# Two reorderings in a two-layer attention and expert kernel: relative scores copied ahead of the later statistics, with identity products on TensorE, and attention outputs copied one place earlier

## The chip, the cores and the metric

The kernel runs on one core of a Trainium2 chip. The metric is the device time of one execution in microseconds (us). A core has TensorE (PE: products; PEld are its weight loads), VectorE (DVE), ScalarE (ACT), GpSimd (POOL) and SyncE (SP, which here only issues DMAs). Each engine works through its own instructions in the order in which they are written, and waits at a semaphore where the program says so. What is late on one engine is therefore late for all that stands behind it there.

## The reference

Two layers over x of 4 x 512 tokens, 256 wide; all in float32.

```python
# layer 0: attention with relative positions, 16 heads of 16 (the "first attention")
q, k, v = nx @ Wq.T + bq, ctx @ Wk.T + bk, ctx @ Wv.T + bv
attn = softmax(causal((q @ k.T + skew(q @ Er.T)) / sqrt(16)))
x = x + attn @ v
# layer 0: causal self-attention (the "second attention"), then 8 experts, top 2
...
# layer 1: cross-attention, 16 heads of 64, no mask (the "third attention")
q, k, v = norm(x) @ Wq, ctx @ Wk, ctx @ Wv
x = x + softmax(q @ k.T / 8) @ v @ Wo + bo
# layer 1: 16 experts, top 6
...
```

The inputs are normalised over the 256 features ahead of each part: mean and variance (statistics), square root, reciprocal, and one subtract-and-multiply.

## The kernel before, in words

The order of the instructions on each engine is written out by hand; semaphores tie the engines.

**Opening** (0 to 53 us of the trace). Tokens come in two loads: `X[:, 0:4]` (tiles 0 to 3, the first batch element) and `X[:, 4:]` (the other 12 tiles, `ld["x1"]`). DVE does the statistics of the first four (`stats_a(0, RT)`), ACT the root (`sqrt_a`), DVE normalises into `nrm`, PE turns them with the identity `idf` (`tokens_a`), ACT copies them to `NT`. PE projects queries (`queries_a(0)`, four products of 128x512), ACT writes them to `QPa`. Then come the relative scores of job 0 and job 1 (a job is four heads of one batch element): `rel_scores_a(n, r)` for r = 0 to 3 makes a group of eight short-contraction products of 128, 256, 384 and 512 columns (L838). Each group is copied out by two engines, half each: `rel_copy_first(n, r)` on ACT (semaphore `a_en`) and on DVE (`a_end`), since PE may write group q only when ACT has copied group q-1 and DVE group q-2. SP writes the copies to DRAM and reads them back skewed. Between the two jobs PE makes the keys (`keys_a(0)`) and the next queries (`queries_a(1)`); then values and more tokens; then the loop over 16 jobs, whose first relative scores are at L873.

**Third attention** (1022 to 1600 us). 32 jobs (a pair of heads of one batch element), each of four row blocks `s = 4m + r`, taken in pairs (r = 0 and r = 2). In a pair PE makes scores of two blocks (`scores_c`), turns the weights of the two blocks before (`transposes_c`), and multiplies values of blocks s-6 and s-5 (`values_c`, L1350), with one projection in between (`to_bank`). The values of a job gather in one bank, `OUT1`; ACT copies it to `O1T` (`outputs_c`, L1856). The first values of a job wait for the copy of the job before (`c_ot`). ACT also does the exponentials (`exp_c`, L1798), copies half of the turned weights (L1808, L1812), and from job 7 on, at the end of the first pair of a job, rounds the weights of a later job (`weights_high`: `WK`, `WQ`, now and then `WV` or the context), and in a few jobs a square root (`sqrt_c`, with a load of its function table). POOL takes the low parts from those (L736). With every fourth job the projection out (`project_out`, L1306) reads `O1T`.

Of the kernel before, what the change touches and what calls it, by code (L numbers as in the profile page):

```python
# [13 lines left out]
P = 128  # L14
# [4 lines left out]
TB = T // P  # L19
RT = S // P  # L20
# [182 lines left out]
def build(nc, A, out):  # L203

    with ExitStack() as ctx:
# [147 lines left out]
        idf = place("idf", [P, P], F32)  # L353
# [18 lines left out]
        PD = [ctx.enter_context(nc.psum_tensor(f"PS{i}", [P, 2, 512], F32)) for i in range(4)]  # L372
# [427 lines left out]
        def _(pe):  # L800
            mm = nc.tensor.matmul
# [17 lines left out]
            def tokens_a(i):  # L819
                bank_a(("l", i))  # L820
                pe.wait_ge(ln_sem[0]["nrm"], 2 * i + 2)
                for k in range(DK):
                    for x in range(2):
                        last = nc.tensor.transpose(MB[:, (2 * k + x) * P:(2 * k + x + 1) * P],
                                                   nrm[:, (2 * i + x) % 4, k * P:k * P + P], idf[:])
                last.then_inc(a_mw, 1)
# [104 lines left out]
            def queries_h(bank, m):  # L931
                b, half = divmod(m, 2)
                return project(bank, lambda k: eight_heads(WFs, k, half), lambda k: NT[:, k, b * S:b * S + S], S)

            tokens_a(0)
            tokens_a(1)
            pe.wait_ge(ld["w0"], 16)
            queries_a(0)
            pe.wait_ge(ld["er"], 32 * HQ)
            pe.wait_ge(a_mr, A_AT["q", 0] + 1)  # L940
            for r in range(RT):
                rel_scores_a(0, r)
# [564 lines left out]
        def _(act):  # L1507
# [3 lines left out]
            def sqrt_a(i, tb0, tb1):  # L1511
                act.wait_ge(ln_sem[0]["var"], i + 1)
                af(sd[:, tb0:tb1], mv[:, tb0:tb1, 1], ACT.Sqrt, bias=eps_c[:, 0:1]).then_inc(ln_sem[0]["sd"], 1)
# [93 lines left out]
            tokens_a(1)  # L1607
            act.wait_ge(s_bp, 3)
            queries_a(0)
            sqrt_a(1, RT, TB)  # L1610
            for r in range(RT):
                rel_copy_first(0, r)
            keys_a(0)
            queries_a(1)
            for r in range(RT):
                rel_copy_first(1, r)
            tokens_a(2)
            tokens_a(3)
# [234 lines left out]
            def outputs_c(m):  # L1853
                b, p = divmod(m, HP)
                act.wait_ge(c_pv, m + 1)
                af(O1T[b % 2][:, p, :], OUT1[:], ACT.Copy).then_inc(c_ot, 1)  # L1856

            def from_bank(use):
                kind, i = use
                if kind == "k":  # L1860
                    keys_c(i)
                elif kind == "m":
                    tokens_c(i)
                elif kind == "n":
                    tokens_d(i)

            for s in range(0, NST, 2):
                uses = C_PAIR[s // 2]
                m, r = divmod(s, RT)
                if r == 2 and m >= 2:  # L1870
                    outputs_c(m - 2)
                early = s < 6 or not first_is_late(s)
                exp_c(s)
                if s >= 2:
                    weights_c(s - 2)
                for use in uses[:1] if early else ():
                    from_bank(use)
                exp_c(s + 1)
                for use in () if early else uses[:1]:
                    from_bank(use)  # L1880
                if s >= 2:
                    weights_c(s - 1, [0])
                for use in uses[1:2] if early else ():
                    from_bank(use)
                if s >= 2:
                    weights_c(s - 1, [1])
                for use in uses[2 if early else 1:]:
                    from_bank(use)
                if s in (12, 20, 28):
                    sqrt_c(3, s // 8 + 1, RT * (s // 8), RT * (s // 8) + RT)  # L1890
                b, w = divmod(m - HP - 1, HP)
                if r == 0 and 0 <= b < B and w == 4:
                    sqrt_c(4, b, RT * b, RT * b + RT)
                for use in _weight_splits(m):
                    if r == (2 if use[0] == "nt" else 0):
                        weights_high(use)
                if m == NC1 - 1:
                    for i in range(2 * (r // 2), min(2 * (r // 2) + 2, B - 1)):
                        high_part(i)
            for s in range(NST, NST + 40):  # L1900
                m, r = divmod(s, RT)
# [16 lines left out]
        def _(dve):  # L1918
# [23 lines left out]
            def normalise_a(i):  # L1942
                if i >= 2:
                    dve.wait_ge(a_mw, A_W["l", i - 2] + 1)
                for tb in (2 * i, 2 * i + 1):
                    v.tensor_scalar(nrm[:, tb % 4], X[:, tb], mv[:, tb, 0:1], rstd[:, tb:tb + 1], ALU.subtract, ALU.mult)\
                        .then_inc(ln_sem[0]["nrm"], 1)
# [18 lines left out]
            rstd_a(0, 0, RT)  # L1966
            normalise_a(0)
            normalise_a(1)
            dve.wait_ge(ld["x1"], 16)
            stats_a(RT, TB)  # L1970
            for r in range(RT):
                rel_copy_first(0, r)
            rstd_a(1, RT, TB)
            normalise_a(2)
            normalise_a(3)
            for r in range(RT):
                rel_copy_first(1, r)
            dve.wait_ge(ld["rows0"], 48)

            def values_a(tb):  # L1980
# [687 lines left out]
```

## Time and profile before

| what | value |
|---|---|
| median of 3 runs | 1799.07 us (1798.94 to 1806.17) |
| the profiled execution | 1804.25 us, span 1802.1 us |
| PE busy | 1638.3 us, 91% of the span |
| DVE busy | 1083.9 us, 60% |
| ACT busy | 897.6 us, 50% |
| POOL busy | 353.9 us, 20% |
| mean granted TensorE clock | 0.971 |

The span runs from the first to the last instruction; 2.15 us of the profiled execution lie around it. The profiled execution is 5.18 us over the median. Busy time of PE is modelled, since its products are pipelined.

### The profile page before, as it was taken

How to read it: one execution, taken by the hardware profiler on the slowest of the kernel's cores; microseconds unless marked ns; L12 is line 12 of the kernel's file. 1: busy time of each engine (PE TensorE's matmuls, PEld its weight loads, DVE VectorE, ACT ScalarE, POOL GpSimd, SP SyncE). 2: the span in 40 equal slices, each digit the busy share in tenths (PEclk: the TensorE clock that was granted, in tenths of full speed). 3: DMA queues.
4: the chain of work that ended last, by engine and by line, in shares of the span. 5: the costliest groups of instructions: out<-in, count | busy, mean ns of one | idle time of the engine just before them, and what ended most of it. 6: DMA issues, size and time to landing. Idle time of an engine off the chain costs nothing.

```text
span 1802.1 us, 32539 instructions
## 1 busy us (share of the span) xinstructions
PE 1638.3 (91%) x11152; PEld 1100.4 (61%) x11153; DVE 1083.9 (60%) x2947; ACT 897.6 (50%) x2088; POOL 353.9 (20%) x405
## 2 busy tenths in 40 slices
PE   4898989988888878999999798999999999998998
PEld 1555555543333366999999444566666666567887
DVE  3666677755555455222222587876876867767776
ACT  2788788635555421443334366755765765630000
POOL 0011111102442121111110331243332322110000
PEclk9999999889999896999999899999999999999999
DMA  7687778500000093111112320100010000020001
GB/s 262 232 289 258 262 259 286 171 7 1 1 1 1 1 322 139 35 37 36 36 37 70 97 65 24 53 24 24 30 30 25 19 24 18 13 82 1 1 0 47
DMA packets 74448, 149.63 MB, mean 83 GB/s; under 512 B 7024, under 2 KB 49648, under 8 KB 69840
## 3 DMA queue, kind: packets, MB, share of 16 engines
q1 hardware_dynamic: 70912, 138.64, 22.8%
q0 software_dynamic: 3408, 9.31, 1.9%
q8 instruction: 76, 1.25, 0.3%
q14 instruction: 52, 0.43, 0.1%
HBM read 96.68 MB, written 51.25 MB: 82 GB/s over the span
## 4 chain that ended last, share of the span: by engine, by line
PE 76%; DVE 9%; ACT 8%; issue 4%; DMA 1%; POOL 0%; SPq 0%; another core or an unknown queue 0%; DVEq 0%; ACTq 0%; POOLq 0%
PE PS L1380 9%; PE PS L1217 8%; PE PS L1202 7%; PE PS L806 7%; PE PS L1335 6%; PE PS L1251 5%; PE PS L1350 5%; PE PS L1012 4%; PE PS L1325 4%; PE PS L873 4%; PE PS L895 4%; PE PS L1306 3%; PE PS L906 2%; PE PS L1032 2%; ACT PTf L1671 1%
## 5 line engine op out<-in xcount | busy, mean ns | idle before, releaser
L1798 ACT ACTIVATE P<-PS,nm 128x512 f32<-128x512 f32 x256 | 174.6, 695 | 105.7 <-DVE nm L2383 91.5
L1335 PEld LDWEIGHTS PS<-idf,P 128*128 128x128 f32 x1024 | 116.5, 142 | 98.1 <-issue 64.7
L2084 DVE CUSTOM_DVE_ANT_0 dump<-PS,maskw 128x256 f32<-128x256 f32 (+3 forms) x256 | 114.8, 488 | 91.9 <-PE PS L1017 86.7
L1995 DVE CUSTOM_DVE_ANT_0 SN<-PS,SR 128x128 f32<-128x128 f32 (+3 forms) x256 | 115.3, 488 | 87.6 <-PE PS L877 87.5
L1335 PE MATMUL PS<-idf,P 128*128 128x128 f32 x1024 | 154.1, 280 | 11.9 <-ACT PTb L1808 8.2
L2383 DVE TENSOR_REDUCE nm<-PS 128x2 f32<-128x1024 f32 x128 | 150.5, 1216 | 21.1 <-PE PS L1325 20.8
L1217 PEld LDWEIGHTS PS<-xT,W1c 128*128 128x128 f32 x1248 | 145.3, 192 | 4.2 <-ACT xT L1724 2.3
L1217 PE MATMUL PS<-xT,W1c 128*128 128x128 f32 x1248 | 145.8, 275 | 1.8 <-ACT xT L1724 1.8
L1202 PE MATMUL PS<-EW,hT 128*128 x624 | 141.2, 379 | 0.0
L1012 PE MATMUL PS<-QP,KP 32*128 32x128 f32 (+3 forms) x512 | 107.7, 494 | 36.8 <-ACT PTf L1671 33.5
L1671 ACT ACTIVATE PTf<-PS 128x512 f32<-128x512 f32 (+3 forms) x256 | 97.9, 435 | 83.0 <-PE PS L1012 82.8
L1551 ACT ACTIVATE SN<-SN,nm 128x128 f32<-128x128 f32 (+3 forms) x256 | 128.8, 555 | 7.8 <-DVE nm L1995 7.7
L2274 DVE TENSOR_TENSOR ysb<-PS,fc2b 128x256 f32<-128x256 f32 x39 | 16.6, 425 | 191.1 <-PE PS L1202 191.1
L1350 PE MATMUL PS<-PTb,V 128*64 128x512 f32 x512 | 124.0, 604 | 7.7 <-ACT O1T L1856 7.6
L1724 ACT ACTIVATE xT<-PS,cols 128x128 f32<-128x128 f32 x78 | 31.5, 454 | 198.2 <-PE PS L1192 198.2
L2603 DVE SCALAR_TENSOR_TENSOR X<-PS,gat,X 128x256 f32<-128x256 f32 x224 | 97.1, 479 | 46.0 <-PE PS L1380 45.1
L1202 PEld LDWEIGHTS PS<-EW,hT 128*128 128x128 f32 x624 | 115.6, 190 | 14.7 <-issue 0.4
L2392 DVE TENSOR_SCALAR P<-P,rc 128x512 f32<-128x512 f32 x256 | 119.8, 510 | 4.3
L873 PE MATMUL PS<-ErP,QPa 32*128 32x128 f32 (+3 forms) x448 | 92.7, 486 | 22.6 <-ACT EN L1544 13.4
L877 PE MATMUL PS<-Ka,QPa 32*128 32x512 f32 (+3 forms) x512 | 108.1, 496 | 2.7 <-DVE nm L1995 2.5
L1017 PE MATMUL PS<-KP,QP 32*128 32x384 f32 (+3 forms) x512 | 104.7, 492 | 4.0 <-DVE MX L2084 2.0
L895 PEld LDWEIGHTS PS<-idf,SN 128*128 128x128 f32 x640 | 69.3, 143 | 61.1 <-ACT SN L1551 37.4
(345 smaller groups left out, 3306.7 us busy)
## 6 DMA issues: line engine op xcount, KB each, us to landing
SR<-rel SPq DMA_DIRECT2D x16, 1024.0 KB, 7.4
rel<-EN SPq DMA_DIRECT2D x15, 1024.0 KB, 4.8
SR<-rel SPq DMA_DIRECT2D x16, 768.0 KB, 5.8
rel<-EN SPq DMA_DIRECT2D x15, 768.0 KB, 4.1
SR<-rel SPq DMA_DIRECT2D x16, 512.0 KB, 4.5
EW<-in_fc1T SPq DMA_DIRECT2D x8, 1024.0 KB, 11.6
EW<-in_fc2T SPq DMA_DIRECT2D x8, 1024.0 KB, 12.2
rel<-EN SPq DMA_DIRECT2D x15, 512.0 KB, 3.3
```

Source lines behind the costliest of these rows:

```text
L806: last = mm(bank[0:m, 0:n], w(k), src(k), start=(k == 0), stop=(k == DK - 1))
L873: rel_mm = mm(PD[0][:, i, 0:w], QPa[e // 2 % 3][o:o + HQ8, r * P:r * P + P], ErP[e % 2][o:o + HQ8, S - w:S], start=True, stop=True)
L895: last = nc.tensor.transpose(TRA[i % 2][:, o:o + P], SN[(2 * t + j) % 6][:, c * P:c * P + P], idf[:])
L1012: keys_mm = mm(STB[(2 * s + x) % 3][:, 0:S - c * P], KP[o:o + HQ8, hg, b * S + c * P:b * S + c * P + P], QP[n % 4][o:o + HQ8, c * P:S], st ...
L1202: last = mm(PS[5][:, 0:D], hT[s][:, f, :], EW[:, bass.ds(e, 1), o:o + D].rearrange("p e d -> p (e d)"), start=(f == 0), stop=(f == FK - 1))
L1217: ins = mm(PS[1 + 2 * s + f // 4][:, f % 4 * P:f % 4 * P + P], W1c[s][:, o:o + P], xT[:, k, :], start=(k == 0), stop=(k == DK - 1), skip_g ...
L1335: last = nc.tensor.transpose(TR1[j][:, c * P:c * P + P], P1[s % 4][:, j, c * P:c * P + P], idf[:])
L1350: last = mm(OUT1[o:o + DH1, :], V1[chunk % NV1][:, m % VG, o:o + DH1], PT1[m % 2][:, j, c, :], start=(c == 0), stop=(c == RT - 1), skip_gr ...
L1380: last = mm(PS[tb % 8][:].rearrange("p (e n) -> p e n", e=2), x[:, k, t], w[i][:, :, k, :], start=(n + k == 0), stop=(n + k == len(parts) ...
L1551: af(sn, sn, ACT.Exp, bias=nm[:, (ku + i) % 16:(ku + i) % 16 + 1], scale=-1.0).then_inc(a_ex, 1)
L1798: last = af(P1[s % 4][:, j, :], PD[s % 2][:, j, :], ACT.Exp, bias=nm1[:, s % 4, j:j + 1], accum_out=sm1[:, s % 4, j:j + 1])
L2383: v.tensor_reduce(nm1[:, s % 4, :], PD[s % 2][:], AX.X, ALU.max, negate=True).then_inc(c_max, 1)
```

## The change

Three engines get another order, and PE gets 22 more products, in four places of the opening. Their result goes to a bank that nobody reads.

```diff
@@ TensorE, opening
+            def keep_warm(count):
+                for _ in range(count):
+                    mm(PD[2][:, 0, 0:P], idf[:], idf[:], start=True, stop=True)
+
+            keep_warm(12)
             tokens_a(0)
+            keep_warm(3)
             tokens_a(1)
+            keep_warm(4)
             pe.wait_ge(ld["w0"], 16)
             queries_a(0)
             pe.wait_ge(ld["er"], 32 * HQ)
+            keep_warm(3)
             pe.wait_ge(a_mr, A_AT["q", 0] + 1)
             for r in range(RT):
                 rel_scores_a(0, r)
@@ ScalarE, opening
             queries_a(0)
-            sqrt_a(1, RT, TB)
             for r in range(RT):
                 rel_copy_first(0, r)
             keys_a(0)
             queries_a(1)
-            for r in range(RT):
+            rel_copy_first(1, 0)
+            sqrt_a(1, RT, TB)
+            for r in range(1, RT):
                 rel_copy_first(1, r)
@@ ScalarE, third attention
                 m, r = divmod(s, RT)
-                if r == 2 and m >= 2:
-                    outputs_c(m - 2)
                 early = s < 6 or not first_is_late(s)
...
                 for use in uses[2 if early else 1:]:
                     from_bank(use)
+                if r == 0 and m >= 2:
+                    outputs_c(m - 2)
                 if s in (12, 20, 28):
@@ VectorE, opening
             normalise_a(1)
+            for r in range(RT):
+                rel_copy_first(0, r)
             dve.wait_ge(ld["x1"], 16)
             stats_a(RT, TB)
-            for r in range(RT):
-                rel_copy_first(0, r)
+            rel_copy_first(1, 0)
+            rel_copy_first(1, 1)
             rstd_a(1, RT, TB)
             normalise_a(2)
+            rel_copy_first(1, 2)
             normalise_a(3)
-            for r in range(RT):
-                rel_copy_first(1, r)
+            rel_copy_first(1, 3)
```

On VectorE at the start of the program, before the change, the statistics of twelve tiles (BN_STATS, BN_AGGR) stand ahead of the four copies of job 0's relative scores (EN), and `nrm` ahead of those of job 1 (PTa):

```order
L1946 TENSOR_SCALAR nrm<-X,mv,rstd 128x256 x4
L1932 BN_STATS st<-X 128x6 x12
L1935 BN_AGGR mv<-st 128x2 x12
L1953 COPY EN_55<-PS 128x256
L1953 COPY EN_56<-PS 128x512
L1953 COPY EN_57<-PS 128x768
L1953 COPY EN_58<-PS 128x1024
L1940 RECIPROCAL rstd<-sd 128x12
L1946 TENSOR_SCALAR nrm<-X,mv,rstd 128x256 x4
L1953 COPY PTa_0_79<-PS 128x256
```

The same place of VectorE with the change (lines have moved by ten):

```order
L1956 TENSOR_SCALAR nrm<-X,mv,rstd 128x256 x4
L1963 COPY EN_55<-PS 128x256
L1963 COPY EN_56<-PS 128x512
L1963 COPY EN_57<-PS 128x768
L1963 COPY EN_58<-PS 128x1024
L1942 BN_STATS st<-X 128x6 x12
L1945 BN_AGGR mv<-st 128x2 x12
L1963 COPY PTa_0_79<-PS 128x256
L1963 COPY PTa_1_80<-PS 128x512
L1950 RECIPROCAL rstd<-sd 128x12
L1956 TENSOR_SCALAR nrm<-X,mv,rstd 128x256 x2
L1963 COPY PTa_2_81<-PS 128x768
```

The statistics have moved behind all four copies of job 0 and the normalising between the copies of job 1; nothing is added or gone.

On TensorE at the start of the program, with the change (L824 are the turned tokens, L806 the projections, L838 the relative scores; L938 is new):

```order
L938 MATMUL PS<-idf 128x128 x12
L824 MATMUL PS<-idf,nrm 128x128 x4
L938 MATMUL PS<-idf 128x128 x3
L824 MATMUL PS<-idf,nrm 128x128 x4
L938 MATMUL PS<-idf 128x128 x4
L806 MATMUL PS<-NT,WAq 128x512 x2
L938 MATMUL PS<-idf 128x128 x3
L838 MATMUL PS<-ErP_89,QPa_61 128x128 x4
```

The 22 identity products have come in; all else on TensorE keeps its order.

On ScalarE in the third attention, in a job that has a square root and three weight copies at the end of its first pair, before the change:

```order
L1808 ACTIVATE PTb_211<-PS 128x4x128
L1812 ACTIVATE PTb_211<-PS 128x4x128
L1817 ACT_TABLE_LOAD
L1817 ACTIVATE sd<-mv,eps_c 128x4
L1754 ACTIVATE WK1h<-WK_180 128x256
L1758 ACTIVATE WQ1h<-WQ_186 128x256
L1769 ACTIVATE WVh<-WV 128x1024
L1856 ACTIVATE O1T_213<-PS 128x512
L1798 ACT_TABLE_LOAD
```

The same place with the change:

```order
L1818 ACTIVATE PTb_211<-PS 128x4x128
L1822 ACTIVATE PTb_211<-PS 128x4x128
L1866 ACTIVATE O1T_213<-PS 128x512
L1827 ACT_TABLE_LOAD
L1827 ACTIVATE sd<-mv,eps_c 128x4
L1764 ACTIVATE WK1h<-WK_180 128x256
L1768 ACTIVATE WQ1h<-WQ_186 128x256
L1779 ACTIVATE WVh<-WV 128x1024
L1808 ACT_TABLE_LOAD
```

The copy of the outputs has moved ahead of the table load, the root and the weight copies, and nothing else has; in jobs that have none of these it stands where it stood.

## Rows read from the trace of the kernel before

**Rows 1.** The page: busy time (share of the span) of PE, chain by engine

```profile
PE 1638.3 (91%) x11152; PEld 1100.4 (61%) x11153; DVE 1083.9 (60%) x2947; ACT 897.6 (50%) x2088; POOL 353.9 (20%) x405
...
PE 76%; DVE 9%; ACT 8%; issue 4%; DMA 1%; POOL 0%; SPq 0%; another core or an unknown queue 0%; DVEq 0%; ACTq 0%; POOLq 0%
```

**Rows 2.** Timeline of the opening: start us, us, engine, line, operation [idle before <-releaser]

```profile
9.36 1.09 PE L824 MATMUL PS<-idf,nrm 128*128 128x128 f32 x4 [9.36 <-DVE nrm L1946]
...
13.02 3.75 PE L806 MATMUL PS<-NT,WAq 128*128 128x512 f32 x4 [0.78 <-ACT NT L1517]
...
17.71 0.81 PE L838 MATMUL PS<-ErP,QPa 32*128 32x128 f32 x8 [0.93 <-ACT QPa L1527]
19.79 4.02 DVE L1932 BATCH_NORM_STATS2 st<-X 128x6 f32<-128x256 f32 x12 [9.94 <-DMA X<-in_x]
...
24.67 0.39 DVE L1953 COPY EN<-PS 128x256 f32<-128x256 f32 x1
...
25.41 1.24 PE L838 MATMUL PS<-ErP,QPa 32*128 32x256 f32 x8 [6.90 <-ACT EN L1523]
...
31.98 3.71 PE L806 MATMUL PS<-CTA,WAk 128*128 128x512 f32 x4
...
33.52 1.38 DVE L1946 TENSOR_SCALAR nrm<-X,mv,rstd 128x256 f32<-128x256 f32 x4
...
37.23 1.98 PE L806 MATMUL PS<-NT,WAq 128*128 128x512 f32 x4 [1.54 <-ACT Ka L1533]
...
39.14 0.50 PE L838 MATMUL PS<-ErP,QPa 32*128 32x128 f32 x8
...
44.62 1.13 PE L806 MATMUL PS<-WAv,CTA 128*128 128x256 f32 x4
...
53.25 0.37 PE L873 MATMUL PS<-ErP,QPa 32*128 32x128 f32 x1
```

**Rows 3.** DMA issues of the opening: KB each, median us to landing

```profile
X<-in_x SPq DMA_DIRECT2D x1, 1536.0 KB, 12.3
...
cols<-in_cols SPq DMA_DIRECT2D x1, 17.0 KB, 3.3
```

**Rows 4.** Busy time, granted clock, DMA share by stretch: opening, first attention, routing

```profile
13.00:17.00 4.00, 3.75 (x4) 1.17 (x4) 0.00 (x0) 0.13 (x1) 0.00 (x0) 1.00 1.04 375
...
320.00:340.00 20.00, 17.91 (x125) 9.58 (x126) 13.16 (x48) 13.17 (x24) 3.19 (x5) 0.73 0.63 222
...
692.00:696.00 4.00, 2.21 (x4) 0.38 (x2) 3.79 (x12) 0.00 (x0) 0.00 (x0) 0.72 0.05 16
```

**Rows 5.** Timeline of PE in the routing stage

```profile
688.71 5.47 PE L1177 MATMUL PS<-idf 128*128 128x512 f32 x6
```

**Rows 6.** Waits of PE in the third attention: us in total, times, longest

```profile
PE PS L1350 <- ACT O1T L1856: 7.6, 8, 1.9
```

**Rows 7.** Timeline of PE in the third attention

```profile
1118.46 1.94 PE L1350 MATMUL PS<-PTb,V 128*64 128x512 f32 x8 [0.99 <-ACT O1T L1856]
1121.60 1.07 PE L1335 MATMUL PS<-idf,P 128*128 128x128 f32 x8 [0.61 <-ACT PTb L1808]
...
1266.29 1.94 PE L1350 MATMUL PS<-PTb,V 128*64 128x512 f32 x8 [1.93 <-ACT O1T L1856]
1269.43 0.63 PE L1360 MATMUL PS<-idf,nrm 128*128 128x128 f32 x4 [1.21 <-DVE nrm L2425]
...
1331.30 3.72 PE L1306 MATMUL PS<-WO,O1T 128*128 128x256 f32 x16 [0.56 <-ACT O1T L1856]
...
1581.62 1.94 PE L1350 MATMUL PS<-PTb,V 128*64 128x512 f32 x8 [1.02 <-ACT O1T L1856]
```

**Rows 8.** Timeline of ACT, POOL and DVE around the wait at 1266

```profile
1262.40 1.28 ACT L1817 ACT_TABLE_LOAD   x1
...
1266.47 2.35 POOL L736 TENSOR_TENSOR WVl<-WV,WVh 128x1024 fp32r<-128x1024 f32 x1
...
1266.48 2.48 DVE L2425 TENSOR_SCALAR nrm<-X,mv,rstd 128x256 f32<-128x256 f32 x1
```

## The prediction

> **What bounds the kernel now.** I read the page first: PE is busy for 91% of the span and makes up 76% of the chain that ended last [rows 1]. So whatever takes PE's idle or slow time away, at a place where nothing else is just behind, shortens the whole by as much. Then I read the two stretches that the diff touches.
>
> In the opening (the timeline) the reader is to see one hole and one slow stretch. The hole: the first group of relative scores ends at 17.71 + 0.81 = 18.52, but its copy starts on DVE only at 24.67, because DVE first waits for the late load of X until 19.79 and then does twelve tiles of statistics; PE starts its second group at 25.41 [rows 2]. The slow stretch: the same kind of projection takes 3.75 at 13.02 and 3.71 at 31.98, but 1.98 at 37.23; the first group of relative scores takes 0.81 at 17.71, and 0.50 at 39.14 [rows 2]. That is the lower of the two clock levels (1.2 GHz) up to about 36 us and the upper (2.4 GHz) after it. The granted clock of the stretch 13 to 17 reads 1.00 [rows 4], which those durations contradict; I go by the durations.
>
> In the third attention (waits, then PE's timeline) PE waits 7.6 us in 8 places for the copy of the outputs [rows 6], and at two places 0.56 more for it at the projection out [rows 7] (the row at 1331.30; the other is its like in the next batch element).
>
> **The change part by part.** The sum is made against the profiled execution, 1804.25 (span 1802.1 and 2.15 around it). The median is 5.18 lower. I don't know where in the program the other executions are faster, and subtract the same amounts from the median.
>
> *Copies ahead of the statistics.* DVE's copy needs group 0 (18.52) and nothing else, so it starts near 18.6 instead of 24.67; on ACT the square root that waited for the same statistics is gone from ahead of the copy too. PE's second group then starts near 19.0, not 25.41: **-6.4**. What is late next? The statistics (4.02, and 0.9 more for their averages until the copy at 24.67) now run behind the copy of group 3. That copy starts about 31.98 - 6.4 = 25.6 in slow clock, near 22.5 in fast; the load has landed at 19.79 in any case [rows 2, 3]. They end near 28.8 in the fast case, when DVE is wanted for job 1's first copy at about 28.5: **+0.2**. The normalising (1.38 for four tiles, so 0.7 for two [rows 2]) goes into DVE's gaps between copies of job 1, where DVE waits for PE: 0. If these gaps were gone it would cost 1.4 and the reciprocal. The square root is one short ACT instruction in such a gap. SP's order is unchanged; each write and read of the relative scores moves earlier with its copy. They share the DMA engines with the end of the load of X; the cover is that what they bring is first used in the loop at 53.25, behind the values and tokens that begin at 44.62, and both move by the same amount.
>
> *The identity products.* The 22 cost at most 1.09 / 4 = 0.27 each at the lower clock, from the four tokens turned at 9.36 [rows 2]. The first twelve (3.2 us) can start when `idf` and `cols` are in, 1.84 (when SP issued `cols`) + 3.3 = 5.2 [rows 3], and end at 8.5, ahead of 9.36: 0. Three between the tokens take 0.8 where PE idled about 0.7 (the second tokens ran from 13.02 - 0.78 - 1.09 = 11.15, the first to 10.45); four ahead of the queries 1.1 against 0.78; three after them 0.8 against 0.93 [rows 2]. Exposed at the lower clock 0.4, at the upper nothing: **+0.2**.
>
> *What they give back.* The trace has no such products at this place, so I bound it. Below: the clock does not rise before the point where it does now, and they give nothing. Above: it is high from 13.02 on. Then the projection saves 3.75 - 1.98 = 1.8. The four groups of job 0 take, without the hole, 1.3 (0.81, a copy of 0.39 and the signals) + (31.98 - 25.41) = 7.9 at the lower level, and those of job 1 take 44.62 - 39.14 = 5.5 at the upper: 2.4 saved. The keys save 3.71 - 1.98 = 1.7 [rows 2]. Together 5.9. The nearest row for when it rises is the routing stage: six identity products of 512 columns run from 688.71 for 5.47, and the granted clock of 692 to 696 is 0.72, so it was 0.5 and rose to 1.0 within that stretch, near 694.2: about 5.5 us after they began [rows 4, 5]. With the change PE has work from 9.36 almost without a gap to 16.8, after 3 us of work before. I take the rise at about 15, half of the projection's share: **-0.9 - 2.4 - 1.7 = -5.0**. Opening in all: -6.4 + 0.2 + 0.2 - 5.0 = **-11.0**; the loop starts near 42.2 instead of 53.25.
> The Trainium skill, "TensorE: Matmul & The Clock Gate", Part 1, says that the slow state is the default which activity releases, and that how many slow products come first differs between executions of the same kernel. By that rule some executions would get the whole 5.9 and some little of it; the sum would be -11.9 to -6. The trace shows a single execution and can't say.
>
> *The outputs' copy.* It now stands ahead of the table load at 1262.40 instead of behind it and the weight copies [rows 8]. It never has to wait there: the weight copy before it already needs PE to be past those values. ACT does the same work between the same two points, so the exponentials come when they came. So only waits with no ACT or DVE wait close behind are won. Of the 7.6 in 8 places, the one at 1118 (0.99) is followed by 0.61 for the turned weights, which hang on the exponentials: that wait just grows. A second such place, in the last batch element, is counted the same. The one at 1266 (1.93, and its like one batch element on) is followed by 1.21 for `nrm` [rows 7]. `nrm` took 2.48 on DVE from 1266.48, beside a POOL subtraction from 1266.47 for 2.35, where 0.35 is usual [rows 2, 8]: it is released at the same time, so PE idles the full 3.1 all the same. This leaves 7.6 - 2 x 0.99 - 2 x 1.93 - 1.02 = 0.7 in three short waits, won whole; of the 1.02 at 1581 I take 0.7, since DVE goes on only after the router's products that stand behind it on PE; and the 2 x 0.56 at the projection out are won: **-2.5**. Bounds: 0 and -8.7 (all ten).
> The Trainium skill, "SBUF — State Buffer", section "SBUF: two separate sides", says that DVE (in its two-port modes) and GpSimd take one shared port pair as an exclusive lock for a whole instruction. By that rule the trace agrees at 1266; if `nrm` were not held, the copy's move would give some 4 us more, near -6.5.
> POOL's inputs come 0.6 later from ACT, but POOL still has the low parts of keys and queries ahead of them: 0.
>
> *Sum:* -11.0 - 2.5 = -13.5: 1790.8 for an execution like the profiled one, 1785.6 from the median. As the faster executions may already lack a little of the slow clock, I say **1786**.
>
> **The rivals.**
> A, *the clock does not rise early.* For it: 13.02 to 16.77 is solid work and didn't raise it [rows 2]. Against it: that was 3.75 us, now it is over 7. Then 6.4 - 0.4 + 2.5 = 8.5 saved: 1790.6.
> B, *the third attention gives nothing*, since PE's short waits turn up again at the next exponential: 11.0 saved, 1788.
> C, *the waits give more*: DVE gets ahead of POOL by the 0.01 us that part them at 1266 [rows 8], 2 us at each of two places: 1782.
> D, *slower*: all later work stands 11 us earlier, and the first attention sits where the clock may fall: in 320 to 340 the grant is 0.73, so 10.8 of 20 us were at the lower level, about 5.4 us lost [rows 4]. If more stretches fall, each costs half its length. From 1786 it would take 45 us more at the lower level to come out over 1808; nothing in the change points there, as PE's work in the loop is the same. One such stretch more gives 1791.
>
> **How the numbers follow.** Chances: the forecast 0.55 (1782 to 1789), A 0.19, B 0.13, C 0.08, D 0.05 (0.03 of it over 1808). About 0.5%, 9 us, is what a measurement of this kernel can tell from no change: faster means under 1790.1. The forecast, C and most of B are faster, A splits at that line (0.06 under), and of all these some 0.03 is lost to a stretch of lower clock: 0.77 faster, 0.20 same, 0.03 slower. The range goes from C less some clock, 1780, to A plus a stretch of lower clock, 1793.5.
>
> **What would show it.** Right: DVE's first EN copy at 18 to 19; no statistics ahead of it; keys_a at about 22.5 taking 2.0; L873 first at 41 to 43; L1350 waiting for O1T nearly nowhere, yet the wait for nrm near its old place grown to about 3. Wrong: keys at 3.7 (A); L873 first after 46; PE's waits for PTb grown by what O1T lost (B); a loss of granted clock between 42 and 600 greater than before (D). The forecast fails most likely on the clock term.

## The result and the profile after

The changed kernel takes 1793.62 us (median of 22 executions, 1783.59 to 1801.14), beside 1801.36 us for the kernel before on the same chip: a ratio of 0.9958 [0.9941, 0.9974], or 7.6 us less. Forecast were 13.5 us less. The gain is clear of the noise, and a little over half of what was forecast. Its profiled execution took 1797.7 us, with a span of 1795.6.

The page of the changed kernel, busy time and chain by engine, to set beside [rows 1]:

```profile
PE 1650.4 (92%) x11196; PEld 1111.3 (62%) x11197; DVE 1084.5 (60%) x2947; ACT 896.9 (50%) x2088; POOL 353.5 (20%) x405
...
PE 78%; DVE 10%; ACT 8%; issue 4%; DMA 1%; POOL 0%; SPq 0%; DVEq 0%; ACTq 0%; POOLq 0%
```

PE's busy time has grown by 12.1 us, though the 22 new products take some 7 of them. Busy time that grows under the same work is time at the lower clock: the mean granted clock is 0.960, and was 0.971. (The 0.971 is a little too high, since the record of that execution reads 1.00 up to 40 us, against the durations there. The run that leaves the opening alone has 0.966.)

The timeline of PE in the opening of the changed kernel, beside [rows 2] (start, us, engine, line, operation, idle before and its releaser; L938 are the identity products, and each shows as two records):

```profile
5.15 4.57 PE L938 MATMUL PS<-idf 128*128 128x128 f32 x24 [5.15 <-DMA cols<-in_cols]
9.55 0.60 PE L824 MATMUL PS<-idf,nrm 128*128 128x128 f32 x4
...
12.28 1.96 PE L806 MATMUL PS<-NT,WAq 128*128 128x512 f32 x4
...
16.07 0.71 PE L838 MATMUL PS<-ErP,QPa 32*128 32x256 f32 x8 [0.50 <-ACT EN L1532]
...
19.36 2.09 PE L838 MATMUL PS<-ErP,QPa 32*128 32x512 f32 x8 [0.93 <-ACT EN L1532]
21.39 3.78 PE L806 MATMUL PS<-CTA,WAk 128*128 128x512 f32 x4
26.70 1.98 PE L806 MATMUL PS<-NT,WAq 128*128 128x512 f32 x4 [1.54 <-ACT Ka L1542]
...
33.03 2.09 PE L838 MATMUL PS<-ErP,QPa 32*128 32x512 f32 x8 [0.93 <-ACT PTa L1532]
35.05 2.07 PE L806 MATMUL PS<-WAv,CTA 128*128 128x256 f32 x4
...
48.34 0.57 PE L873 MATMUL PS<-ErP,QPa 32*128 32x128 f32 x1
```

The same opening by stretches (columns: length; busy us and instructions of PE, PEld, DVE, ACT, POOL; granted clock; DMA share; GB/s):

```profile
17.00:19.00 2.00, 0.93 (x8) 0.31 (x8) 1.05 (x2) 0.95 (x2) 0.00 (x0) 0.95 1.10 348
19.00:21.00 2.00, 1.64 (x8) 0.52 (x8) 0.46 (x1) 0.31 (x1) 0.00 (x0) 0.50 0.97 191
...
27.00:31.00 4.00, 2.83 (x20) 1.00 (x18) 1.51 (x12) 1.63 (x4) 0.35 (x1) 1.00 0.95 342
...
35.00:50.00 15.00, 11.63 (x40) 7.00 (x40) 4.90 (x13) 3.00 (x5) 1.27 (x2) 0.50 0.69 245
```

The hole is gone: the second group starts at 16.07 instead of 25.41. The clock rises before 9.55 (the turned tokens take 0.60, against 1.09 before), earlier than I thought. But it falls twice: by 19.36 (2.09 for the last group of job 0, where 1.14 is usual at the upper level, then keys 3.78), and again by 33.03, and from 35 to 50 it reads 0.50. There the four projections of values take 2.07 each, where the kernel before needed 1.13. The loop starts at 48.34 instead of 53.25: 4.9 us won, not 11.0.

In the third attention the waits for the outputs' copy of [rows 6] are gone. PE's waits for `nrm` have grown. Over the whole run they were 4.2 us in 3 places, the longest 1.8, and are now:

```profile
PE PS L1369 <- DVE nrm L2437: 9.3, 4, 3.2
```

The timelines of ACT, POOL, DVE and PE at the two places that answer to 1266 in [rows 7, 8]:

```profile
1255.53 0.59 ACT L1866 ACTIVATE O1T<-PS 128x512 f32<-128x512 f32 x1
1256.14 1.28 ACT L1827 ACT_TABLE_LOAD   x1
...
1259.71 2.34 POOL L736 TENSOR_TENSOR WVl<-WV,WVh 128x1024 fp32r<-128x1024 f32 x1
...
1259.72 2.81 DVE L2437 TENSOR_SCALAR nrm<-X,mv,rstd 128x256 f32<-128x256 f32 x2
...
1262.67 0.63 PE L1369 MATMUL PS<-idf,nrm 128*128 128x128 f32 x4 [3.20 <-DVE nrm L2437]
...
1405.55 1.09 PE L1369 MATMUL PS<-idf,nrm 128*128 128x128 f32 x4 [3.21 <-DVE nrm L2437]
1406.43 1.91 PE L1344 MATMUL PS<-idf,P 128*128 128x128 f32 x8
```

The copy is early, and PE stands still just as long: 1.93 + 1.21 has become one wait of 3.20, as forecast. The new thing is behind the second one: 1.09 instead of 0.63, and 1.91 for what takes 1.04 behind the first. The clock has fallen: it reads 0.51 over the 6 us behind this wait.

### The profile page after: what moved, and what is told of

Its sections match the earlier page's. It is cut to its first block, busy times and chain, and to the rows that moved or that the text cites. A ratio compares the mean times of both kernels' runs of the same rounds, so it can differ in the third digit from the quotient of the medians.

```text
span 1795.6 us, 32625 instructions
## 1 busy us (share of the span) xinstructions
PE 1650.4 (92%) x11196; PEld 1111.3 (62%) x11197; DVE 1084.5 (60%) x2947; ACT 896.9 (50%) x2088; POOL 353.5 (20%) x405
## 4 chain that ended last, share of the span: by engine, by line
PE 78%; DVE 10%; ACT 8%; issue 4%; DMA 1%; POOL 0%; SPq 0%; DVEq 0%; ACTq 0%; POOLq 0%
PE PS L1389 9%; PE PS L1226 8%; PE PS L806 8%; PE PS L1211 8%; PE PS L1344 6%; PE PS L1260 5%; PE PS L1359 5%; PE PS L1334 5%; PE PS L1021 4%; PE PS L873 4%; PE PS L895 4%; PE PS L1315 3%; PE PS L906 2%; PE PS L1041 2%; ACT PTf L1681 1%
## 5 line engine op out<-in xcount | busy, mean ns | idle before, releaser
L2615 DVE SCALAR_TENSOR_TENSOR X<-PS,gat,X 128x256 f32<-128x256 f32 x224 | 97.1, 479 | 46.1 <-PE PS L1389 45.3
L1359 PE MATMUL PS<-PTb,V 128*64 128x512 f32 x512 | 124.0, 605 | 0.0
L873 PE MATMUL PS<-ErP,QPa 32*128 32x128 f32 (+3 forms) x448 | 93.6, 490 | 23.0 <-ACT EN L1553 13.3
L1026 PE MATMUL PS<-KP,QP 32*128 32x384 f32 (+3 forms) x512 | 104.7, 492 | 4.0 <-DVE MX L2096 2.0
```

Of the source, the lines that this page charges most:

```text
L873: rel_mm = mm(PD[0][:, i, 0:w], QPa[e // 2 % 3][o:o + HQ8, r * P:r * P + P], ErP[e % 2][o:o + HQ8, S - w:S], start=True, stop=True)
L1359: last = mm(OUT1[o:o + DH1, :], V1[chunk % NV1][:, m % VG, o:o + DH1], PT1[m % 2][:, j, c, :], start=(c == 0), stop=(c == RT - 1), skip_gr ...
```

## The experiments

Each kernel is timed beside the kernel before on the same chip. "Loop" is the start of the loop over the 16 jobs, the first product of L873 in the one profiled execution, in us (kernel before: 53.25, and 52.1 in the run that leaves its opening alone, so 52.7 in the mean). The last column is the mean granted clock from 13 to 25 us, 25 to 40 and 40 to 55.

| kernel | ratio, 95% interval | loop | granted clock |
|---|---|---|---|
| changed | 0.9958 [0.9941, 0.9974] | 48.3 | 0.74, 0.73, 0.57 |
| changed, second time | 0.9960 [0.9937, 0.9983] | 42.1 | 0.86, 1.00, 0.89 |
| copies alone | 0.9937 [0.9916, 0.9959] | 45.2 | 0.79, 0.94, 0.89 |
| copies alone, second time | 0.9966 [0.9949, 0.9984] | 44.9 | 0.77, 0.95, 0.89 |
| identity products alone | 0.9997 [0.9979, 1.0016] | 53.5 | 0.83, 0.68, 1.00 |
| outputs alone | 0.9998 [0.9981, 1.0016] | 52.1 | 0.79, 0.71, 0.97 |
| copies and identity products | 0.9958 [0.9933, 0.9984] | 48.5 | 0.76, 0.73, 0.56 |
| copies and outputs | 0.9963 [0.9947, 0.9978] | 44.9 | 0.77, 0.96, 0.89 |
| first half of the gaps filled | 0.9964 [0.9945, 0.9983] | 46.7 | 1.00, 0.70, 0.61 |
| all gaps filled | 0.993 [0.991, 0.995] | 40.4 | 1.00, 1.00, 1.00 |
| all filled, `nrm` earlier | 0.993 [0.9906, 0.9953] | 40.4 | 1.00, 1.00, 1.00 |
| all filled, outputs as before | 0.9924 [0.9905, 0.9943] | 40.6 | 1.00, 1.00, 1.00 |
| changed, WVl in four parts | one execution | 42.3 | 0.86, 1.00, 0.89 |

**Each part alone.** The copies ahead of the statistics, without the other two parts:

```diff
-            keep_warm(12)
             tokens_a(0)
-            keep_warm(3)
             tokens_a(1)
-            keep_warm(4)
...
-            keep_warm(3)
...
+                if r == 2 and m >= 2:
+                    outputs_c(m - 2)
...
-                if r == 0 and m >= 2:
-                    outputs_c(m - 2)
```

> The opening's new order on DVE and ACT, without the 22 identity products and with the outputs' copy at its old place. Theory 1 (the hole of 6.9 us is what the reordering is worth; the lower clock in the opening costs the rest): the second group of relative scores starts near 19.0 instead of 25.4, the query projection still takes 3.7; first product of the loop near 47, thus 6 us earlier; time ratio about 0.9965. Theory 2 (the identity products are what moves the opening): less than 3 us earlier at the loop, ratio 0.999.

Measured 1795.4 us beside 1804.39, ratio 0.9937. This part carries the whole gain. Its opening, PE's timeline in the second such run (the first is like it: 45.2 and 44.9 at the loop):

```profile
13.01 3.49 PE L806 MATMUL PS<-NT,WAq 128*128 128x512 f32 x4 [0.78 <-ACT NT L1522]
17.43 0.50 PE L838 MATMUL PS<-ErP,QPa 32*128 32x128 f32 x8 [0.93 <-ACT QPa L1532]
18.43 0.71 PE L838 MATMUL PS<-ErP,QPa 32*128 32x256 f32 x8 [0.49 <-ACT EN L1528]
19.86 1.66 PE L838 MATMUL PS<-ErP,QPa 32*128 32x384 f32 x8 [0.72 <-ACT EN L1528]
22.45 2.09 PE L838 MATMUL PS<-ErP,QPa 32*128 32x512 f32 x8 [0.93 <-ACT EN L1528]
24.47 2.90 PE L806 MATMUL PS<-CTA,WAk 128*128 128x512 f32 x4
...
44.94 0.37 PE L873 MATMUL PS<-ErP,QPa 32*128 32x128 f32 x1
```

Here too the clock is up at 17.43 (0.50), without any identity product. It is down by 19.86 (1.66 for a group that takes 0.93 at the upper level), and up again within the keys (2.90, between 1.98 and 3.78). The values run at the upper level. The second timing:

> The reordered copies alone, a second time. Theory 1: the ratio of 0.9937 seen before holds within its interval (0.992 to 0.996) and is not above that of the full change by more than 0.001; loop start 44 to 46.5 us if the clock rises at the same place as before, up to 49 if the level differs between executions as it did with the full change (48.3 and 42.1). Rival (the first result was a lucky draw and the identity products do matter): 0.997 or more.

1794.12 us, 0.9966. The two intervals overlap, and both hold the full change's 0.9958.

The 22 identity products on the order of before:

```diff
+            keep_warm(12)
             tokens_a(0)
+            keep_warm(3)
...
```

> The 22 identity products alone, in the order of the kernel before. Theory 1: the query projection takes 2.0 instead of 3.75, but its 1.8 us are swallowed by the wait for the statistics (the copy stays at 24.7), and the clock falls in that wait of 9 us or more, so that groups 1 to 3 and the keys run at the lower level as before: loop start at 53.2 give or take 1, ratio 1.000. Theory 2: 4 us or more earlier, ratio 0.9975.

Ratio 0.9997, loop at 53.5. PE's timeline around the old hole:

```profile
16.11 0.50 PE L838 MATMUL PS<-ErP,QPa 32*128 32x128 f32 x8 [0.17 <-ACT QPa L1536]
26.65 1.24 PE L838 MATMUL PS<-ErP,QPa 32*128 32x256 f32 x8 [10.03 <-ACT EN L1532]
```

The first group is 1.6 earlier and at the upper level, and behind a hole of 10.03 all of it is lost.

The outputs' copy alone, on ACT only:

```diff
-                if r == 2 and m >= 2:
-                    outputs_c(m - 2)
...
+                if r == 0 and m >= 2:
+                    outputs_c(m - 2)
```

> Only the copy of the outputs moved, the opening as before. Theory 1 (short waits are won, the long ones become a single wait of 3.2 for nrm): waits for O1T gone, waits for nrm up from 2.4 to about 7.5, the third attention 1.8 to 2.5 us shorter if the clock holds, up to 2 less if it falls behind one of the 3.2 us waits; ratio 0.9985 to 1.000. Theory 2 (all ten waits are won): 8 us shorter, ratio 0.9955.

Ratio 0.9998. The waits for O1T are gone and those for `nrm` grow to 9.3 us in 4 places, as in the changed kernel. Nothing is won that the time shows; its interval leaves room for 3.4 us at most.

**Two parts at a time.** The full change without the outputs' part, and without the identity products:

```diff
+                if r == 2 and m >= 2:
+                    outputs_c(m - 2)
...
-                if r == 0 and m >= 2:
-                    outputs_c(m - 2)
```

> The change without its third-attention part: copies ahead of the statistics and the 22 identity products, outputs copied where they were. If the outputs' move is worth nothing (theory 1: its saved waits of 7.6 us come back as a wait for nrm and as lower clock behind it), this equals the full change: ratio 0.994 to 0.997 against before, loop start anywhere from 42 to 48 us, the wait for the outputs' copy again about 7.6 in 8 places, the wait for nrm 2 to 2.4 in 2 places, clock 1.00 behind both. If the move is worth its forecast 2.5 us (rival), this is 0.0014 above the full change's 0.996, which five rounds can hardly tell; if it costs time, this is 2 to 4 us faster, about 0.993.

```diff
-            keep_warm(12)
...
-            keep_warm(3)
...
-            keep_warm(4)
...
-            keep_warm(3)
```

> The change without the identity products. Theory 1 (the reordered copies carry the gain, identity products in these four places add under 2 us): ratio 0.994 to 0.997, loop start 44 to 46.5 us, q projection about 3.7 us at the lower clock, keys either level. Rival (the identity products carry the clock part of the forecast, 5.0 us): 0.998 to 0.999 here.

The ratios are 0.9958 and 0.9963, each the same as the full change within its interval. Neither the identity products nor the outputs add anything that can be measured to the copies.

**The same kernel again.** The changed kernel was timed and profiled a second time, with no edit.

> The changed kernel once more, unaltered, on another occasion. Theory 1 (after the first fall the clock of the opening is a matter of where the waits lie to the moment at which the clock is reviewed, and so of luck): its opening shows another pattern of falls, and the loop starts anywhere between 43 and 49 (48.3 before). Rival (the pattern belongs to the kernel): loop at 48.3 within 0.3 and the same granted clock in 25 to 40 and 40 to 55 (0.73, 0.57).

Ratio 0.9960, the same. But the profiled execution differs from the first. PE's timeline:

```profile
19.86 2.09 PE L838 MATMUL PS<-ErP,QPa 32*128 32x512 f32 x8 [0.93 <-ACT EN L1532]
21.88 2.67 PE L806 MATMUL PS<-CTA,WAk 128*128 128x512 f32 x4
...
32.41 1.14 PE L838 MATMUL PS<-ErP,QPa 32*128 32x512 f32 x8 [0.93 <-ACT PTa L1532]
33.48 1.13 PE L806 MATMUL PS<-WAv,CTA 128*128 128x256 f32 x4
...
42.10 0.37 PE L873 MATMUL PS<-ErP,QPa 32*128 32x128 f32 x1
```

The same program, the same waits, and another clock. Against the first profile the keys take 2.67 instead of 3.78 (1.1 us), the last group 1.14 instead of 2.09 (0.95), four values 1.13 instead of 2.07 (3.8), and two groups of tokens 0.66 instead of 1.12 (0.9). That is 6.75, less the 0.5 by which this execution was behind at 19.86: the 6.2 between 48.3 and 42.1. Four profiled executions have this opening (the two of the changed kernel, the one of copies and identity products, and the one with WVl in four parts). Their loops start at 48.3, 42.1, 48.5 and 42.3, 45.3 in the mean. The three without identity products (copies alone twice, copies and outputs) start the loop at 45.2, 44.9 and 44.9. So the identity products at these four places bring the clock up sooner, and it then falls at the last group of job 1, ahead of the values, in two profiled executions of four; in the mean they give nothing.

**All gaps filled.** If the clock falls in the idle gaps between the short groups, then more identity products there must keep it. 41 more, into a bank that nobody reads at that time, behind each group but the last of a job, behind the keys, behind each projection of values and between the tokens:

```diff
+            def fill(count):
+                for _ in range(count):
+                    mm(PS[6][:, 0:P], idf[:], idf[:], start=True, stop=True)
...
             for r in range(RT):
                 rel_scores_a(0, r)
+                fill((2, 3, 4, 0)[r])
...
             keys_a(0)
+            fill(7)
             queries_a(1)
             for r in range(RT):
                 rel_scores_a(1, r)
+                fill((3, 3, 4, 0)[r])
...
                 values_to_bank_a(tb)
+                fill(3)
             tokens_a(2)
+            fill(3)
```

> The changed kernel with more identity products, into a bank that nothing reads before the loop, in every gap of PE from the first group of relative scores to the last tokens before the loop (2, 3, 4 behind the groups of job 0, 7 behind the keys, 3, 3, 4 behind those of job 1, 3 behind each of the values, 3 between the tokens). Theory 1 (the forecast of 11 us failed because the clock fell at 19 and again at 33, in the gaps between short groups): the clock now stays up, the keys take 2.0, the values 1.1 each, the loop starts at 42 to 43.5 instead of 48.3, and the time is 4 to 6 us below the changed kernel's, ratio to the kernel before 0.993. Rival (the gaps are not what lowers it, or the loads of the masks are late at the loop): loop starts after 46, ratio 0.996 or more.

Ratio 0.993. PE's timeline:

```profile
19.40 1.14 PE L838 MATMUL PS<-ErP,QPa 32*128 32x512 f32 x8
20.47 1.99 PE L806 MATMUL PS<-CTA,WAk 128*128 128x512 f32 x4
...
31.73 1.13 PE L806 MATMUL PS<-WAv,CTA 128*128 128x256 f32 x4
...
40.36 0.37 PE L873 MATMUL PS<-ErP,QPa 32*128 32x128 f32 x1
```

From 13 us to the loop everything runs at the upper level. The loop starts at 40.4, 40.4 and 40.6 in the three kernels that have this opening, earlier than expected and with little scatter. That is 12.2 us ahead of before, of which the copies alone give 7.7 and the identity products, all of them together, 4.5. In the time the fills show less clearly: this ratio is not apart from that of the copies alone on the same chip, 0.9937. But the three filled kernels have 0.9928 in the mean, and the six with the copies and open gaps 0.9957, which makes 5 us, about what the loop shows.

Only the fills of the first half, against the kernel with all of them:

```diff
                 fill((2, 3, 4, 0)[r])
...
             keys_a(0)
             fill(7)
...
-                fill((3, 3, 4, 0)[r])
...
-                fill(3)
             tokens_a(2)
-            fill(3)
```

> The change plus identity products in the gaps between the groups of job 0 and ahead of the keys and the next queries, none in the gaps of job 1 and later. Theory 1 (the clock falls only in gaps left idle): clock 1.00 to about 29 us, keys about 2.0 us, loop start 40.4 if it then lasts, up to 46 if it falls in the gaps of job 1 (values 2.1 each instead of 1.1). Rival (once up for long enough it stays up whatever the gaps): 40.4 exactly as with all gaps filled. Ratio 0.992 to 0.995.

Ratio 0.9964. The granted clock reads 1.00 in every stretch from 13 to 29, and it is down behind the first gaps that are left open:

```profile
31.42 2.09 PE L838 MATMUL PS<-ErP,QPa 32*128 32x512 f32 x8 [0.93 <-ACT PTa L1539]
33.44 2.07 PE L806 MATMUL PS<-WAv,CTA 128*128 128x256 f32 x4
...
46.72 0.58 PE L873 MATMUL PS<-ErP,QPa 32*128 32x128 f32 x1
```

What was at the upper level without a break until then still fell, in gaps of 0.62, 0.72 and 0.93. In other executions the same gaps of job 1 did no harm (42.1 above), so they let the clock fall in some and not in all.

**The wait for `nrm`.** POOL's subtraction WVl cut into four instructions of 256 columns:

```diff
-            def low_part(parts):
+            def low_part(parts, cuts=1):
...
+                if cuts > 1:
+                    for k in range(DK):
+                        for x in range(cuts // DK):
+                            c = slice(x * VG * P * DK // cuts, (x + 1) * VG * P * DK // cuts)
+                            last = nc.gpsimd.tensor_tensor(low[:, k, c], full[:, k, c], high[:, k, c].bitcast(F32), ALU.subtract)
...
+                              4 if kind == "wv" else 1)
```

> The changed kernel, with POOL's subtraction for the low part of the value weights cut from one instruction of 2.35 us into four of about 0.6. Theory 1 (the single wait of 3.2 for nrm that took the place of the waits for the outputs is DVE held by POOL's instruction): nrm takes 1.0 or less instead of 2.5, PE's longest wait for nrm falls from 3.2 to 1.0 to 1.8, the waits for nrm in the third attention from 7.5 to 4 or less. Rival (nrm waits for the square root on ACT or for DVE's own order): still 3.2 and 7.5.

One execution, 1800.28 us. Timelines of DVE, POOL and PE:

```profile
1263.37 1.61 DVE L2445 TENSOR_SCALAR nrm<-X,mv,rstd 128x256 f32<-128x256 f32 x2
...
1263.38 2.87 POOL L740 TENSOR_TENSOR WVl<-WV,WVh 128x256 fp32r<-128x256 f32 x4
...
1265.12 0.63 PE L1377 MATMUL PS<-idf,nrm 128*128 128x128 f32 x4 [2.01 <-DVE nrm L2445]
1266.33 1.94 PE L1352 MATMUL PS<-idf,P 128*128 128x128 f32 x8 [0.58 <-ACT PTb L1826]
```

Two `nrm` take 1.61 instead of 2.81, and PE waits 2.01 instead of 3.20, still longer than expected. DVE does wait for the end of the POOL instruction that it meets, so it is POOL that holds `nrm`. But the 1.2 us won are half eaten by the next wait, for PTb, and the clock falls behind both waits all the same (0.72 and 0.54 in the 6 us after them). On the filled kernel, `nrm` was put ahead of the copy of PTb on DVE:

```diff
+                    normalise_of(s)
...
-                    normalise_of(s)
```

> The kernel with the filled gaps, and DVE's root reciprocal and nrm in the third attention put ahead of its copy of turned weights, so that they start before POOL's long subtraction. Theory 1: nrm takes 0.4 again, the single waits of 3.2 for it shrink to under 1.2, the clock doesn't fall behind them, third attention 4 to 6 us shorter than with filled gaps alone, ratio to the kernel before 0.990. Rival (PE then waits for the turned weights or the exponentials instead): waits for PTb grow by as much, ratio 0.993 as with filled gaps alone.

Ratio 0.993, no better. DVE and POOL:

```profile
1253.86 3.15 DVE L2447 TENSOR_SCALAR nrm<-X,mv,rstd 128x256 f32<-128x256 f32 x2
...
1253.78 0.72 POOL L736 TENSOR_TENSOR WQ1l<-WQ,WQ1h 128x256 fp32r<-128x256 f32 x1
1254.47 2.39 POOL L736 TENSOR_TENSOR WVl<-WV,WVh 128x1024 fp32r<-128x1024 f32 x1
```

The first `nrm` now meets WQ1l and the next WVl: 3.15 instead of 2.81, and PE waits 2.94. My fix failed, and the clock falls behind both of these waits too (0.72 and 0.74). The last kernel is the filled opening with the outputs' copy where it was:

```diff
+                if r == 2 and m >= 2:
+                    outputs_c(m - 2)
...
-                if r == 0 and m >= 2:
-                    outputs_c(m - 2)
```

> The kernel with the filled gaps, but the outputs' copy at its old place. Theory 1 (the move wins 2 us of short waits and gives about that back where two waits join into one of 3.2 and the clock falls): the third attention within 2 us of that with the move, ratio within 0.001 of 0.993. Rival (the move is worth 2.5 or more): 0.9945 or above.

1790.62 us beside 1804.68, ratio 0.9924. It is the best of all by its ratio, though not apart from the other two filled kernels. Its third attention is no shorter than theirs (546.2 against 543.5 and 543.7, from the first values to the first experts), so what its profile has ahead of them was not won by the copy's old place there.

## Why the prediction was wrong

**The failed step is the clock term, "-0.9 - 2.4 - 1.7 = -5.0".** It asked when the clock rises and took it for granted that it then stays up. The rise came before 9.55 instead of at 15, better than forecast. What failed is the second half. With gaps of 0.5, 0.7 and 0.9 us between short groups, each group taking a microsecond or less, the clock was down by 19.4 in the first profile, so the last group of job 0 and the keys were as slow as in rival A. In two profiles of four it fell again by 33, on values which had run at the upper level before. No term of my sum had these falls. The opening gave 4.9 in the one profile of the changed kernel and 11.1 in the other (forecast 11.0), so the 11.1 is luck and not a hit. Over the four profiles of this opening it gave 52.7 - 45.3 = 7.4. The copies alone give 7.7, so of the 5.0 that the identity products were to bring, nothing is left. The filled kernels, which keep the clock, gave 12.2. The trace of before could have raised the question: from 25.41 the groups of job 0 stayed at the lower level with gaps of 0.7 and 0.9 between them, and those of job 1 stayed at the upper with the same gaps. I read only the second.

**The Trainium skill had a part of the warning.** "TensorE: Matmul & The Clock Gate", Part 1, says that the number of slow products that come first differs between executions. The runs agree: the first twelve identity products took from 4.32 to 5.49 us. But the 6.2 us between 42.1 and 48.3 come from products that turned slow later. I cited the scatter and gave it no weight in the sum. A range for the opening from -6 to -12 with its middle as the forecast would have given -9.

**The copies' term, "-6.4", was right**, if anything small: the copies alone bring the loop from 52.7 to 45.0, 7.7 us. The 1.3 more come from the clock. The run of the outputs alone, with the order of before, has its first group at the upper level too (0.50 at 17.68) and the next, behind the hole, at the lower (1.24 at 24.89); with the hole gone that group takes 0.71. So the clock needed no identity products to be up at 17.4, and it needed the hole to go to be still up one group later.

**"+0.2" for the statistics and 0 for normalising and root: right.** DVE's timeline in the changed kernel:

```profile
22.66 4.00 DVE L1942 BATCH_NORM_STATS2 st<-X 128x6 f32<-128x256 f32 x12
26.70 0.90 DVE L1945 BATCH_NORM_AGGREGATE mv<-st 128x2 f32<-128x6 f32 x12
29.19 0.42 DVE L1963 COPY PTa<-PS 128x256 f32<-128x256 f32 x1 [1.58 <-PE PS L838]
```

The averages end at 27.6, and the first copy of job 1 waits for PE, not for them. Where all gaps are filled and the keys are fast, the averages end at 26.70 and the copy starts at 26.62, 0.2 behind the end of its group at 26.41: the 0.2 of the fast case.

**"+0.2" exposed for the identity products: right in this profile, with a wrong price.** The first twelve took 4.57 us, not 3.2, and the tokens came at 9.55 instead of 9.36. My 0.27 each came from the turned tokens, which show as one record each where an identity product shows as two. Where the clock rose late, the twelve took 5.49 and the tokens came at 10.42, 1.1 us late.

**The outputs' term, "-2.5", was wrong: nothing that can be told from 0.** Take the stretch from the first product of L1359 (the values, L1350 in the kernel before) to the first of the experts. It took 543.5 in the mean of six profiles with the move (541.0 to 548.8) and 543.3 in the mean of six without it (540.6 to 546.2). With this scatter the two means can't be told apart below some 3 us, so the lengths alone don't exclude even the 2.5. Two things speak against it.

*The waits came back.* At 1266 the mechanism was right to 0.1 us: one wait of 3.2 where two of 1.93 and 1.21 were. Elsewhere I counted too much as won. In this stretch PE stands idle for 22.7 us in the mean of the six with the move and 23.5 in that of the six without. The waits for the copy, 8.7 us or more, are gone. But the waits for `nrm` go from 2.4 or less to 7.5, and in three of the six those for the turned weights (PTb) go to between 10.7 and 11.7, where the kernels without the move have 6.6 to 8.2. The longest such wait, before and in the run with the outputs' part alone:

```profile
1082.61 1.07 PE L1335 MATMUL PS<-idf,P 128*128 128x128 f32 x8 [1.31 <-ACT PTb L1808]
```

```profile
1083.25 1.07 PE L1335 MATMUL PS<-idf,P 128*128 128x128 f32 x8 [2.84 <-ACT PTb L1808]
```

*The clock falls more often.* In the 6 us behind the join, over eight profiles with the copy moved (waits of 3.2, and of 2.0 and 2.9 in the two experiments on `nrm`), the granted clock was below 0.8 in 11 of 16 places. Over the six with the copy where it was, it was 0.97 or more behind the second wait in all 12, but in two of these it had fallen behind the first, as in the run of the identity products alone, where the values take 3.43 instead of 1.94 and the 6 us from there read 0.72:

```profile
1266.58 3.43 PE L1359 MATMUL PS<-PTb,V 128*64 128x512 f32 x8 [1.92 <-ACT O1T L1865]
```

So it is 11 of 16 against 2 of 12. A clock of 0.73 over 6 us is 1.6 us lost at most, one of 0.51 is 2.9. PE's busy time in the stretch is 520.8 in the mean with the move and 519.9 without: 0.9 more, against 0.7 less of idle time. That it is the length of the wait, and not what comes behind it, was argued from these counts and not tried by itself.

Together -7.4 + 0 stands beside the 7.6 measured. That it fits so closely is luck, as other stages move by some us between profiles (the last section). Of the some 6 us that were missing, the opening has 3.6 (the 5.0 of the clock term, less what the copies gave more) and the outputs' term 2.5. The measured 1793.62 lies just above the upper end of the range, 1793.5; my sum started from 1799.07, the median of three executions, where 22 of the same kernel give 1801.36.

**Rival A** was half right (the slow keys, but not for its reason), **rival B** (nothing in the third attention) holds, in part by PTb as it said and in part by the clock. **C** didn't happen: DVE comes 0.01 behind POOL in the new order too, and with WVl in four parts it starts 0.01 ahead (1263.37 against 1263.38) and is held all the same. **D** was named for the loop; the clock fell, but in the opening itself. My sign "L873 first after 46" is what the first profile showed.

**What stays open.** Why the clock falls at 33 in one execution and not in another of the same program with the same gaps, and which of the gaps of job 1 does it. No run has the fills without the 22 identity products ahead of them, so whether these are needed is not known.

## What to carry to other kernels

A forecast of TensorE's clock needs two questions: when it rises, and whether each later gap lets it fall. Where short groups alternate with copies by other engines, fill every gap or expect the level to differ between executions; filler products at the start alone bought nothing here, and fillers in all gaps gave, with those, 4.5 us more than the copies alone, in each of three profiles. Before joining two short waits into a long one, look at the clock behind it: the sum of the waits can fall while the time stays.

## What the runs showed of the hardware

- Twelve identity products of 128x128 had raised the clock within 4.4 us of their start (5.15 to 9.55) in the first profile of the changed kernel. In two others of the nine profiles that begin with them it was still low 5.2 us after their start (the tokens at 10.42 and 10.28 took 0.78). Without them it was up at 17.4 to 17.7, from the tokens at 9.4 on, in four profiles of other kernels, and not yet (0.81 for the first group) in that of [rows 2].
- Two profiled executions of one program differ by 6.2 us at the start of the loop, by the clock alone.
- Gaps of 0.5 to 0.9 us between the groups of job 0 had the clock down by the last group in 7 of 7 profiles in which the hole was gone and these gaps were open. In the open gaps of job 1 it fell in 3 of 11, all three with identity products ahead.
- The first attention's length goes in steps of 3 us, by the clock in two short stretches. From the loop's start to the second attention's first scores (L1026): 322.5 us where the granted clock reads 0.91 in both 165 to 185 and 245 to 265 (both profiles of the changed kernel), 319.6 where it is 0.91 and 1.00 (copies alone, second time), 316.6 where both are 1.00 (all filled, outputs as before). The kernel before had 320.6 and 319.5 with its outputs' part alone changed. All six profiles with the 22 identity products and open gaps in job 1 had 322.3 to 322.6, and so had one of the three with the copies and without these products. That the change adds some 2 us here is possible and not shown.
- Two DVE instructions of 0.35 us each, which meet a POOL instruction of 2.34, take 2.81; cut in four parts, it holds them for 1.61; where each of the two meets a POOL instruction of its own, 3.15. The Trainium skill, "SBUF — State Buffer", "SBUF: two separate sides", says that DVE in a two-port mode and GpSimd share a pair of ports which one of them holds for a whole instruction. The trace agrees in all three; which mode these DVE instructions run in, it doesn't show.
- In float32 each identity product of 128x128 shows as two records. Twelve of them took 5.49 us where all ran at the lower level, 0.46 each. At the upper level three take 0.83 and four 1.06, so 0.23 for each one more.
